# Two-layer decoder on one core, attention over past states: each half's maxima product between the other half's score products, and the value products two steps behind

## The reference

```
rq = heads(output @ Wrq + brq)              # 16 batches x 128 queries
rk = heads(past @ Wrk + brk);  rv = heads(past @ Wrv + brv)     # 2 pasts x 256 keys
rscores = einsum('bhsd,pbhtd->pbhst', rq, rk) * SCALE
rctx = einsum('pbhst,pbhtd->pbhsd', softmax(rscores), rv)
recursive_output = merge(rctx).mean(axis=0)
gate = sigmoid(concat(output, recursive_output) @ Wg + bg)
output = output * (1 - gate) + recursive_output * gate
```

## Time and profile before

| | |
|---|---|
| median of 3 runs | 694.74 us (694.24 to 697.02) |
| the profiled execution | 693.0 us, its span 691.2 us |
| mean granted TensorE clock | 0.942 |
| busy over the span: PE, DVE, ACT, POOL | 80%, 67%, 51%, 28% |
| the stage over past states | from about 141 us (first scores) to about 369 us |

### The profile page before, as it was taken

How to read it: one execution, slowest core, us unless ns; L and a number is a source line. 1 busy time by engine, 2 the same in 40 slices (tenths; PEclk the granted TensorE clock), 3 DMA queues, 4 the chain that set the end, 5 groups by cost and what they waited for, 6 DMA issues and landing times.

```text
span 691.2 us, 14380 instructions
## 1 busy us (share of the span) xinstructions
PE 555.0 (80%) x5354; PEld 305.0 (44%) x5354; DVE 466.3 (67%) x1059; ACT 354.3 (51%) x593; POOL 195.3 (28%) x321
## 2 busy tenths in 40 slices
PE   2687777779999999999984467787799997879785
PEld 0354454223333333333332245565443345779774
DVE  3555665468788887888833658675566764896786
ACT  2255655157777767777783255655111115425762
POOL 5112201060101011010112212135044427485632
PEclk9999999579999999999996699999899999989999
DMA  5338440010001001000011223211555560001001
GB/s 159 99 100 226 125 124 2 1 47 2 2 2 48 2 1 48 2 2 2 1 48 46 73 82 94 56 41 32 183 193 182 198 211 0 1 1 39 10 16 47
DMA packets 44546, 44.08 MB, mean 64 GB/s; under 512 B 6903, under 2 KB 35319, under 8 KB 44343
## 3 DMA queue, kind: packets, MB, share of 16 engines
q1 hardware_dynamic: 42460, 42.01, 21.0%
q10 hardware_dynamic: 2016, 1.15, 0.7%
HBM read 25.18 MB, written 1.18 MB: 38 GB/s over the span
## 4 chain that ended last, share of the span: by engine, by line
PE 52%; ACT 14%; DVE 13%; issue 10%; DMA 5%; ACTq 3%; POOL 3%; SPq 1%; DVEq 0%; POOLq 0%
PE banks L1042 9%; ACT probs L644 7%; PE banks L505 6%; PE banks L984 5%; PE banks L1547 5%; PE banks L424 4%; DVE rec_negmax L1201 4%; PE banks L1024 4%; ACT o_T L1136 3%; ACTq L671 2%; PE banks L1053 2%; DMA past_mem<-gates 2%; PE banks L490 2%; PE banks L467 1%; ACT neg_T L666 1%
## 5 line engine op out<-in xcount | busy, mean ns | idle before, releaser
L1201 DVE TENSOR_REDUCE rec_negmax<-banks 128x2 bf16<-128x512 f32 x256 | 164.4, 688 | 50.4 <-PE banks L984 47.6
L1129 ACT ACTIVATE probs<-banks 128x1024 f32<-128x1024 f32 x128 | 131.2, 1025 | 44.8 <-PE banks L1024 44.7
L782 DVE TENSOR_REDUCE negmax<-banks 128x8 bf16<-128x1024 f32 x64 | 78.3, 1223 | 58.2 <-PE banks L467 58.2
L1042 PE MATMUL banks<-probs,past_mem 128*32 128x256 f32 x1024 | 82.7, 394 | 12.8 <-ACT o_T L1136 12.0
L644 ACT ACTIVATE probs<-banks 128x1024 f32<-128x1024 f32 x64 | 65.5, 1024 | 45.5 <-PE banks L490 30.4
L984 PE MATMUL banks<-shared 62*128 62x512 bf16 x256 | 69.5, 404 | 5.4 <-DVE rec_negmax L1201 5.4
L505 PE MATMUL banks<-probs,shared 128*32 128x128 f32 x1024 | 44.0, 293 | 35.7 <-ACT probs L644 35.5
L1547 PE MATMUL banks<-shared,w_r 128*128 128x512 f32 x128 | 61.9, 619 | 5.9 <-DVE shared L1661 5.6
L1024 PE MATMUL banks<-shared 64*128 64x256 bf16 x512 | 56.5, 277 | 2.7 <-DMA shared<-rec_neg_T 2.7
L1266 POOL TENSOR_TENSOR rctx<-o 128x64 f32<-128x64 f32 x32 | 10.2, 319 | 157.6 <-DVE o L1218 157.6
L1661 DVE TENSOR_TENSOR shared<-past_mem,out_T 128x512 f32<-128x512 f32 x64 | 42.7, 693 | 16.7 <-DMA past_mem<-gates 15.8
(11 more groups left out here) (258 smaller groups left out, 1012.7 us busy)
## 6 DMA issues: line engine op xcount, KB each, us to landing
past_mem<-gates SPq DMA_DIRECT2D x64, 256.0 KB, 5.0
shared<-qk_parts SPq DMA_DIRECT2D x90, 128.0 KB, 2.5
shared<-past_mem SPq DMA_DIRECT2D x30, 128.0 KB, 2.5
xk_T<-in_x_T SPq DMA_DIRECT2D x4, 256.0 KB, 3.3
w_r<-in_w_r SPq DMA_DIRECT2D x1, 1024.0 KB, 6.0
shared<-rec_neg_T SPq DMA_DIRECT2D x64, 2.0 KB
xk_T<-in_ctx_T SPq DMA_DIRECT2D x4, 256.0 KB, 3.1
past_mem<-in_ctx_T SPq DMA_DIRECT2D x8, 128.0 KB, 2.1
```

Of the source, the lines that this page charges most:

```text
L782: nc.vector.tensor_reduce(c.negmax[:, i % 2, :].rearrange("p (r j) -> p r j", r=2)[:, :, 4 * half:4 * half + 4], c.max_pair.rearrange("p ( ...
L1042: last = self.nc.tensor.matmul(c.ctx_bank[HV * q:HV * (q + 1), past * PAIR:(past + 1) * PAIR], c.rV[:, t, 4 * g + q, :], c.probs[:, i % 4, ...
L1129: nc.scalar.activation(c.probs[:, i % 4, :], c.score_pairs[i % 2], ACT.Exp, scale=HEAD_SCALE)\
L1201: self.nc.vector.tensor_reduce(out, c.max_banks[r].rearrange("p (a t) -> p a t", a=NP_PAST), AX_X, ALU.max, negate=True).then_inc(s["rec_m ...
```

## The change

TensorE's stream alone changes. `scores` gets an argument `more`; between the two score products of half r it now issues the maxima product of the other half, 1 - r. In `run` the values product moves from behind both halves' scores to between them, and it is now that of step i - 2. `ahead` still rises by one a step. At the end two values products (steps 14 and 15 of the last pair) stand behind the last scores instead of one.

```diff
-    def scores(self, n, k, r):
+    def scores(self, n, k, r, more):
...
                                          c.QT[64 * r:64 * r + 64, (n // 2) % 2, 2 * g + a,
                                               (n % 2) * PAIR:(n % 2 + 1) * PAIR], start=True, stop=True)
+            if a == 0 and more:
+                self.max_scores(self.ahead, 1 - r)
         last.then_inc(s["rec_score"], 1)
...
                 more = self.ahead < ALL_STEPS
-                self.scores(n, k, 1)
-                self.scores(n, k, 0)
-                if i:
-                    self.values((i - 1) // STEPS, (i - 1) % STEPS)
-                if more:
-                    self.max_scores(self.ahead, 0)
-                    self.max_scores(self.ahead, 1)
-                    self.ahead += 1
+                self.scores(n, k, 1, more)
+                if i >= 2:
+                    self.values((i - 2) // STEPS, (i - 2) % STEPS)
+                self.scores(n, k, 0, more)
+                self.ahead += more
                 if i == 0:
                     self.turn_max(0, 1)
...
         n = NPAIR - 1
+        self.values(n, STEPS - 2)
         self.values(n, STEPS - 1)
         self.turn_ctx(n, 3)
```

## The result

Four runs with the change took 673.12 to 678.93 us, median 675.84; four of the kernel before, 695.46. The ratio is 0.9718, 95% interval 0.967 to 0.9766: 2.8% faster, and clear of the 0.5%. The forecast was 674, with a range of 663 to 691. The profiled execution took 675.13 us, its span 673.3.

A forecast was written before the change was run, and what follows sets the result against it. No engine was full; PE was stuck 4.3 of 28.2 us a pair, behind the values bank's copy and DVE's reductions. Saving 3.0 over 7.06 pairs, 21 us, takes 694.7 to 673.7, said as 674; range 663 to 691.

The forecast's parts named there:

- Work on PE costs as before: Score products beside a maxima product on the other half: still 0.32 us into the values, 0.23 into another block.
- d: Extra length in us of a block on PE if score and maxima products don't overlap; up to 0.21.
- The slower rival: The two kinds of product don't overlap on PE: 23.9 + 32d a pair, 30.6 at 0.21, 712 us; 9%.
- No third turn is saved: Four old score products take 0.40 us, already two turns of 256 columns, so no further gain from a shorter block.
- A group of four steps, 6.03, and 25.2 a pair: Steps k = 5 to 8 take 6.03 us, 24.1 a pair; plus 0.7 and 0.4 makes 25.2 instead of 28.2.
- the walk: Step-by-step timing of k = 5 to 8 with durations from the old trace; 667 to 681 us at 60%.
- The signs that it named: Changed trace: gates 25.2 us apart, DVE's wait under 15, only k = 6 values copy-held, values 0.32 to 0.33 behind blocks.
- Order of waits, "the long wait for M1 is gone": Second maxima product, now spread from the first, no longer waits for two reductions in a row; bare-step limit 1.22 us.
- the two stalls of before: Old kernel's PE: values waiting for the bank's copy, 0.67 us over 0.32; second maxima product waiting for DVE's reductions.
- The first steps count nothing: Five first steps of the stage, in a stretch at a mean clock of 0.58: no gain counted.
- The last ten steps, nothing: Steps without maxima products: PE's cost as before, ACT sets the pace, no gain taken.
- Sum, 21: Whole stage: 7.06 pairs x 3.0 = 21 us saved, 694.7 - 21 = 673.7, said as 674.

The follow-up runs named there:

- the sub-steps: Parts of the change on the old kernel: values two back, 692.09 us; maxima products between the scores, 684.75; both, values behind both halves, 677.04.
- the first experiment: Kernel before, old order of a step, with the values product of step i - 2 in place of i - 1: 692.09 us, ratio 0.9938.
- The mirror image: Changed kernel with transposes and gate product moved between the two halves' blocks and the values of step i - 2 behind both: 734.98 us, ratio 1.0604.

## Why the prediction was right

A pair, step by step, in the runs:

| order | us a pair |
|---|---|
| before | 28.2 |
| values two back alone | 27.7 |
| maxima products between the scores alone | 27.1 |
| both, values behind both halves | 26.0 |
| the change (and values between the halves) | 25.3 |
| ... with lighter reductions | 24.6 |
| ... with the values one back | 40.5 |
| values between the halves, maxima a pair | 29.5 |
| the change with the same half's maxima product | 29.55 |

- *Work on PE costs as before*: right. Blocks take 0.32 and 0.23, also in the new form. The run with the same half gives d = 0.22. The slower rival named what happens if the overlap is missing, and priced it too high: 23.9 + 32d would be 30.9 a pair, measured 29.55, since neighbouring blocks on different halves still overlap.
- *No third turn is saved*: right. The rule of the Trainium skill's page "TensorE: Matmul & The Clock Gate", Part 3 (The mechanism), by which old scores would start strictly in program order, would have given a shorter block. This case's traces do not agree with it: the distance to the values is 0.32 before and after, and in the run with the values alone between the halves one maxima product starts 0.22 ahead of another that stands before it in the program (216.57 and 216.79).
- *A group of four steps, 6.03, and 25.2 a pair*: the sum is right, its terms are not, and that they cancel is luck. The distances between values products are the same in each of four pairs looked at. Where nothing waits they are 1.11 in a bare step (seen in the run with lighter reductions), 1.42 with `turn_max`, 1.80 with `turn_ctx`, 1.58 with `turn_sum` or `turn_out`, 2.27 with the gate. So `turn_sum`, `turn_out` and the gate cost PE 2.1 a pair; the walk hid two of them wholly in stalls and counted 0.7. The waits on top are 1.4 a pair: 0.14 at the first blocks of k = 5, 9 and 13, 0.52 at that of k = 1 (behind VectorE's statistics, for which the walk counted 0.4), 0.33 in k = 2, 0.13 in k = 6. The walk had 4 x 0.57 + 0.4 = 2.7, most of it in k = 6, 10, 14 and 2. What is left of its mechanism is that late reductions are the larger part of the waits, some 1.0 of 1.4; the rest are copies on ScalarE.
- *The signs that it named*: DVE's wait, the distance of the gates and of the values (0.31 to 0.34 in 102 of 108 steps) came as said, and exponentials are over 0.5 behind the second block in 28 of 109 steps, not in most. The values of k = 6 as the only ones held by the copy did not come: six are held in the stretch, one a pair, in k = 2 (243.59).
- *Order of waits, "the long wait for M1 is gone"*: right in effect. But the two stalls of before are one ring, as the sub-steps show: 0.5 and 1.1 alone, 2.2 together. The walk had both edits in it, so it did not need them to add up; adding up the stalls of its rows, 2.7 for the copy and 1.6 for the second maxima product as the first experiment did, would have given 4.3.
- *The first steps count nothing*: mis-sized. The first gate product is 6.3 us earlier, 5.4 without the 0.9 from ahead of the stage. 25 steps lie ahead of it; 20 of them at 3.0 a pair give 3.8. By this estimate the five cold steps gained some 1.6.
- *The last ten steps, nothing*: wrong by 1.5 us, as the change alone loses there; the prediction had seen that neighbouring halves can pair up, and not that a transpose stands between them in six of ten steps.
- *Sum, 21*: 22.3 at the last maxima product, 20.8 at the last values product, 19.6 in the medians.

Why the last 0.7 us (26.0 to 25.3) comes with the values between the halves is seen in the traces, but no run isolates it. In the change a maxima product stands on each side of a transpose, and the values in the other gap, so VectorE gets work in both; its waits are 5.6 us, with the values behind both halves 13.2. There both blocks behind each `turn_max` wait for reductions, 0.50 four times a pair, where the change loses 0.14 three times and 0.52 once. The mirror image, meant to test it, was spoiled by the bank.

## What to carry to other kernels

Where two single-buffered products and their consumer form a ring with a softmax, walk through one whole period with the durations of the rows; stalls in it don't add up, and removing one may give under a quarter. When a pair of products that fill the two halves of the array is split, put something on the other half at each split, and treat the stretches where that partner runs out apart. A walk whose sum meets the measurement can still have its terms wrong: compare the terms, step by step, with the new trace before the same walk is used again. Before an instruction is moved forward on one engine, ask what its bank's last reader has to finish first in its own order.

## What the runs showed of the hardware

- A product on 64 rows beside one of another kind on the other 64 starts within 0.01 us of it, also when its weight load carries a semaphore wait that is already met (226.90 and 226.91). The same products on one half need 0.22 us more when no block on the other half stands next to them.
- A product on a free half can start ahead of one that stands before it in the program and waits for its half: two maxima products in the run with the values alone between the halves (216.57 and 216.79), in 38 of 94 steps, as read there.
- The granted clock in 155 to 325 us was 1.00 in the change (PE's matmuls busy 167 us), 0.79 with the values one back (129), 0.94 in the mirror image (140), and 1.00 with the transposes ahead of the values (126). The busy total alone does not order them, and no run here shows what does.
